# Graph attention on one core: the context is divided on VectorE, and every load and store stands between the transfers of two groups

## The reference, cut to what matters

```python
q = _heads(x @ Wq + bq); k = _heads(x @ Wk + bk); v = _heads(x @ Wv + bv)
scores = jnp.einsum('bhqd,bhkd->bhqk', q, k) / np.sqrt(64)
bias = jnp.where(adj, 0.0, -9e15)[:, None]
probs = jax.nn.softmax(scores + bias, axis=-1)
ctx = jnp.einsum('bhqk,bhkd->bhqd', probs, v)          # then heads side by side
x = _layernorm(x + (ctx @ Wf + bf), axis=-1)
```

## Time and profile before

| | |
|---|---|
| median of 3 runs | 1295.83 us (1287.64, 1295.83, 1299.62) |
| profiled execution | 1290.07 us |
| its span in the trace | 1288.3 us |
| mean granted clock of TensorE | 0.974 of full speed |
| busy: TensorE, VectorE, ScalarE, GpSimd | 92%, 76%, 63%, 44% |
| queue 1 (SyncE's), share of the 16 DMA engines | 76.7% |

### The profile page before, as it was taken

The page is one execution under the profiler, slowest core; times in us unless marked ns, Lnnn a source line. Parts: engine busy times, 40 slices in busy tenths (PEclk is TensorE's granted clock), DMA queues, the critical chain, the costliest instruction groups (busy, mean ns, idle before and its releaser), DMA issues.

```text
span 1288.3 us, 24781 instructions
## 1 busy us (share of the span) xinstructions
PE 1187.8 (92%) x8790; PEld 891.4 (69%) x8790; DVE 984.5 (76%) x1535; ACT 807.7 (63%) x1628; POOL 560.8 (44%) x943
## 2 busy tenths in 40 slices
PE   6998999899998899988999989998999889999874
PEld 5866777566776677766787667776777667786653
DVE  5788877778677886878868878688876778778782
ACT  5666765657665676666666676666775657656551
POOL 1234643446524454344543544344643436433432
PEclk9999999999998999989999999999999989999998
DMA  5688787977879777888778888789787887878784
GB/s 161 154 202 228 181 206 189 230 195 176 204 189 237 180 185 196 194 214 203 188 195 194 220 203 210 180 207 239 182 201 199 207 204 174 212 172 203 193 201 109
DMA packets 111611, 251.71 MB, mean 195 GB/s; under 512 B 27904, under 2 KB 62336, under 8 KB 111488
## 3 DMA queue, kind: packets, MB, share of 16 engines
q1 hardware_dynamic: 107296, 243.58, 76.7%
q10 hardware_dynamic: 4192, 6.56, 1.9%
HBM read 36.11 MB, written 12.58 MB: 38 GB/s over the span
## 4 chain that ended last, share of the span: by engine, by line
PE 55%; SPq 17%; DVE 12%; DMA 7%; ACT 4%; issue 4%; POOL 1%; ACTq 0%; POOLq 0%; DVEq 0%
PE context_ps L538 19%; SPq L308 16%; PE score_ps L523 13%; PE job_ps L425 7%; DMA prob_t<-prob 6%; PE job_ps L427 6%; PE job_ps L426 6%; DVE prob L735 6%; DVE prob L728 4%; ACT prob L628 3%; PE job_ps L459 2%; DVE res L750 1%; SPq L388 1%; PE job_ps L435 0%; PE score_ps L435 0%
## 5 line engine op out<-in xcount | busy, mean ns | idle before, releaser
L728 DVE CUSTOM_DVE_ANT_0 prob<-score_ps,mask 128x1024 f32<-128x1024 f32 x384 | 454.8, 1222 | 225.1 <-PE score_ps L523 163.5
L628 ACT ACTIVATE prob<-prob,row_min 128x1024 f32<-128x1024 f32 x384 | 440.2, 1148 | 213.3 <-DVE row_min L728 212.5
L735 DVE STREAM_TRANSPOSE prob<-prob 128x1024 f32<-128x1024 f32 x384 | 457.8, 1230 | 38.8 <-ACT prob L628 38.8
L538 PE MATMUL context_ps<-prob_t,v_all 128*64 128x256 f32 x3072 | 373.0, 398 | 61.9 <-DMA prob_t<-prob 61.8
L538 PEld LDWEIGHTS context_ps<-prob_t,v_all 128*64 128x64 f32 x3072 | 239.4, 144 | 166.9 <-issue 82.1
L850 POOL TENSOR_TENSOR context<-context_raw,context 128x256 f32<-128x256 f32 x96 | 70.8, 738 | 337.5 <-ACT context_raw L645 337.1
L523 PE MATMUL score_ps<-k_hi,q_hi 64*128 64x512 f32 x768 | 141.1, 445 | 4.5 <-DVE row_min L728 3.6
L425 PE MATMUL job_ps<-xt_hi,weight_hi 128*128 128x256 f32 (+1 forms) x423 | 142.0, 336 | 0.0
L427 PE MATMUL job_ps<-xt_hi,weight_lo 128*128 128x256 f32 (+1 forms) x423 | 135.6, 320 | 0.0
L426 PE MATMUL job_ps<-xt_lo,weight_hi 128*128 128x256 f32 (+1 forms) x423 | 135.5, 320 | 0.0
L523 PE MATMUL score_ps<-k_lo,q_hi 64*128 64x512 f32 x768 | 120.9, 392 | 0.0
(11 more groups left out here) (78 smaller groups left out, 1659.5 us busy)
## 6 DMA issues: line engine op xcount, KB each, us to landing
prob_t<-prob SPq DMA_DIRECT2D x1528, 128.0 KB, 2.4
res<-in_x_dram SPq DMA_DIRECT2D x32, 384.0 KB, 4.3
out_dram<-res SPq DMA_DIRECT2D x32, 384.0 KB, 2.9
adj_in<-in_adj_dram SPq DMA_DIRECT2D x31, 256.0 KB, 3.0
x_in<-in_x_dram SPq DMA_DIRECT2D x16, 384.0 KB, 3.5
x_in<-in_x_dram ACTq DMA_DIRECT2D x14, 384.0 KB, 4.5
prob_t<-prob ACTq DMA_DIRECT2D x8, 128.0 KB, 4.8
res<-in_x_dram SPq DMA_DIRECT2D x1, 768.0 KB, 6.8
```

The source lines that it names most:

```text
L538: last = pe.matmul(context_ps[64 * head:64 * head + 64, 0:GQ], v_all[:, kt, col:col + HS], keys, start=(kt == 0), stop=(kt == TT - 1))
L628: nc.scalar.activation(probabilities(t), probabilities(t), ACT.Exp, scale=-1.0, bias=row_min[:, ring:ring + 1], accum_out=row_sum[:, s // ...
L728: nc.vector.tensor_tensor_reduce(probabilities(t), in_quarters(score_ps[:, head, :]), in_quarters(mask[:, s % 2, :]), 1.0, HUGE, ALU.add, ...
L735: nc.vector.transpose(probabilities(t), probabilities(t)).then_inc(squared, 1)
```

## The change

Two things change.

First, the division of the context. ScalarE no longer copies the product out of PSUM, and GpSimd no longer multiplies: VectorE multiplies straight out of PSUM (`divide`), between the slot's two turns. The tile `context_raw` and the semaphore `context_out` go; the next mix waits for `context_done`, the end of the multiplication.

Second, the places of loads and stores. All four tables now hold even slots only, and the two x loads that ScalarE issued are entries 12 and 14 of `X_LOADS`, on SyncE's queue.

```diff
-STORES = {1: -2, 9: -1, 13: 0, 21: 1}
-RES_LOADS = {2: 0, 10: 1, 14: 2, 22: 3}
-X_LOADS = {4: (0, 0), 6: (0, 1)}
-RESIDUALS = {2: -1, 6: 0, 13: 1, 17: 2}
+STORES = {2: -2, 10: -1, 16: 0, 20: 1}
+RES_LOADS = {4: 0, 12: 1, 18: 2, 22: 3}
+X_LOADS = {4: (0, 0), 6: (0, 1), 12: (1, 0), 14: (1, 1)}
+RESIDUALS = {2: -1, 6: 0, 14: 1, 20: 2}
...
             def mix(b, group):
-                pe.wait_ge(context_out, at(b, GROUPS, group + 2))
+                pe.wait_ge(context_done, at(b, GROUPS, group + 2))
...
-            def take_context(b, group):
-                act.wait_ge(mixed, at(b, GROUPS, group + 3))
-                act.wait_ge(context_done, at(b, GROUPS, group + 2))
-                nc.scalar.activation(context_raw[:], context_ps[:, 0:GQ], ACT.Copy).then_inc(context_out, 1)
...
                     for job in slot_work(b.mode, s):
-                        if job[0] == "m":
-                            take_context(b, job[1])
-                        elif job[0] != "p" and job not in early:
+                        if job[0] not in "pm" and job not in early:
                             evict(b, job)
-                            if job == ("x", FT - 1, 0, 1):
-                                for i in range(2):
-                                    load_x(nc.scalar, b, 1, i)
...
+            def divide(b, group):
+                dve.wait_ge(mixed, at(b, GROUPS, group + 3))
+                dve.wait_ge(job_out, out_through(b, ("i", group, 0, 0)))
+                nc.vector.tensor_tensor(context[:], context_ps[:, 0:GQ], context[:],
+                                        ALU.mult).then_inc(context_done, 1)
...
                         turn_squares(b, 2 * s)
+                    for job in work:
+                        if job[0] == "m":
+                            divide(b, job[1])
+                    if s < SLOTS:
                         turn_squares(b, 2 * s + 1)
...
-            def divide(b, group):
-                pool.wait_ge(context_out, at(b, GROUPS, group + 3))
-                pool.wait_ge(job_out, out_through(b, ("i", group, 0, 0)))
-                nc.gpsimd.tensor_tensor(context[:], context_raw[:], context[:], ALU.mult).then_inc(context_done, 1)
...
                     for job in work:
-                        if job[0] == "m":
-                            divide(b, job[1])
                         if job[0] in "kqx":
                             low_part(b, job)
```

More of the change, by code:

```diff
@@ L157, in graph_attention @@
         raw = sb("raw", [P, 2, 512], F32)
-        context_raw = sb("context_raw", [P, GQ], F32)
         context = sb("context", [P, GQ], F32)
@@ L207, in graph_attention @@
         mixed = sem("mixed")
-        context_out = sem("context_out")
         context_done = sem("context_done")
@@ L419, in _ @@
             pe.sem_inc(mixed, 2)
-            pe.sem_inc(context_out, 2)
             pe.sem_inc(projected, 4)
@@ L702, in _ @@
             dve.sem_inc(masked, 2)
+            dve.sem_inc(context_done, 2)
             dve.sem_inc(sum_done, 8)
@@ L818, in _ @@
             pool.sem_inc(context_lo_done, 1)
-            pool.sem_inc(context_done, 2)
             pool.sem_inc(normalised, 4)
```

## The result

| | before | after |
|---|---|---|
| median | 1297.72 us (4 runs, 1287.64 to 1301.90) | 1260.56 us (4 runs, 1256.01 to 1262.70) |
| profiled execution | 1290.07 us | 1262.70 us |
| its span | 1288.3 us | 1260.9 us |
| mean granted clock | 0.974 | 0.982 |

The ratio is 0.972, 95% interval 0.9656 to 0.9784: faster. The forecast was 1248 with a range of 1234 to 1279. The median lies in the range, 12.6 us above the forecast. So the profiles account for 27.4 us of spans, while the medians differ by 37.2.

A forecast was written before the change was run, and what follows sets the result against it. Bound: TensorE's work plus about 12 us per element of waits for transfer landings and half clock. Six middle elements save 37 us, the last 5, element 0 nothing: 42 off 1290.1 gives 1248 us, range 1234 to 1279.

The forecast's parts named there:

- The two x loads, 3.9 us, and little when ahead of a group: Slot 11, during group 4: ScalarE's loads delay its landing 3.9 us; ahead of a group, its issue time covers them.
- rival B: x loads cost the same wherever placed: 3.9 us in seven elements, 1275 us; sign: landings over 3 us; chance 0.13.
- The store, 0.7 us: A store inside a group's transfers costs it 0.7 us, four times per element; groups 4 and 6 are on the loop.
- A clean group, 12.6 us: An undisturbed group of transfers takes 12.6 us from first issue to landing, ends 12.3 and 12.9.
- The loop walked anew, 7.6 us in element 1: Groups 4 to 7 of batch element 1 recomputed: slot 18's mix starts at 285.4 instead of 292.96, 7.6 us earlier.
- 149.7 us for a middle element: Each of six middle elements: 149.0 us from the walk, plus 0.3 for slot 8 and 0.4 for half clock.
- rival A: New waits in slots 14 and 16 drop TensorE to 1.2 GHz in each element: 20 us, 1268 us; chance 0.14.
- What an element took before doesn't matter: Middle elements: each takes 149.0 us before additions, whatever it took before, since its waits are replaced.
- Element 0 and the last, 0 and -5 us: Element 0 gains 0; the last gains 5 us, from a last turn some 4 us earlier and a shorter end.
- The multiplication, 0.45 us, almost hidden: VectorE between a slot's turns: 0.45 us, 12 per element, leaving it 0.1 us late instead of waiting.
- Rival C: SyncE's queue of all loads, stores and transfers becomes the bound: 161.5 us per element, 40 us slower, 1330; chance 0.07.
- Expected waits of 25 us: TensorE's waits for transfers fall from 61.8 to about 25 us, most in slots 14 and 16.

The follow-up runs named there:

- The queue's half alone: Kernel before with all four new tables and the x loads on SyncE's queue, division as it was: 1262.71 us, ratio 0.9753.
- the small loads: Kernel after with the x loads of slots 12 and 14 cut to 16 of their 128 partitions: 1254.93 us, ratio 0.9688.

## Why the prediction was right, and where it was off

*What bounds the kernel, and where the gain comes from*: shown. The queue's half alone gives the gain to within the noise (1262.71 against 1260.56 us), the division none. Slot 12's wait fell from 4.86 to 0.63 us in element 1 and is at most 1.1 in the other middle elements.

*The two x loads, 3.9 us, and little when ahead of a group*: shown in the main. Near the end of a group one costs 2 us; ahead of one or right behind it the mask or mix starts 1.8 to 1.9 us behind the last issue in most groups. It is not always free: the mix that waits for group 6, with two loads ahead, starts 2.9 us behind the last issue in element 1 and 3.4 in element 3. The second is over the 3 us that I had named as a sign of rival B, the only one in slots 16 and 18 of the middle elements, and with the small loads it went (though element 5 then had 3.0). The loads also cost more before than I had read: group 5, with none of them near its end, landed 3.3 to 3.8 us behind its last issue in every middle element, and 1.7 to 1.8 after the change. TensorE came later than that in five of the six and waited 1.35 us in element 5; the walk's 12.6 us for group 5 holds only because the loads went.

*The store, 0.7 us*: its size is as read, but it is not additive with the loads, by the race above.

*A clean group, 12.6 us*: right on the mean, with a spread that I had not priced. From first issue to mix or mask, groups 4, 5 and 6 of element 1 took 13.1, 12.65 and 12.9 us. The issues alone take 10.0 to 11.9 us, and SyncE starts group 6 up to 1.5 us late. A late landing costs TensorE, and an early one gives nothing back.

*The loop walked anew, 7.6 us in element 1*: 6.4 (156.6 to 150.2). Counted from the element's start, the mixes of slots 12, 14, 16 and 18 start at 78.2, 89.7, 102.1 and 114.5, where the walk had 77.8, 89.1, 100.9 and 113.3. The new waits are there as forecast, in slots 14 and 16, but the second is 2.0 us, not 1.2.

*The step that was mis-sized: 149.7 us for a middle element.* They took 151.8. TensorE's busy time in the six is 144.6 us where the clock stays up, and 9.8 us more in all because it fell in four of them. I had allowed 0.4 us for each, 2.4 in all: **7.4 us** too little. The rest, 6 x 2.1 - 7.4 = **5 us**, is idle time of TensorE: 5.6 us per element, where the walk leaves 149.3 - 144.6 = 4.7. The half clock is half of rival A: it wanted 20 us in seven elements, and the clock took about 9.8 in six. My reason against it was one wait of 1.41 us that left the clock up; waits of 2.04 (element 1) and 2.31 us did so too after the change, but one of 1.08, one of 2.26 and another of 2.04 (element 4, slot 14) ended at 1.2 GHz. The length of the wait ahead of the mix alone does not separate them, and what does stays open. The sum also leans on one profiled execution: it takes 42 us off 1290.1, and by the spans of the two profiles the gain is 27.4. That the medians differ by 37.2 helped the forecast; it was not reckoned.

*What an element took before doesn't matter*: borne out by this pair of profiles. The middle elements took 151.5 to 158.5 us before and take 149.8 to 153.6; element 5, the fast one before (151.5), lost 2.1.

*Element 0 and the last, 0 and -5 us*: -0.7 and -4.1. The 1.6 us ahead of element 0 come with a stretch of 3.4 us at 1.2 GHz, from 20.8 us on. The division-only kernel, with the old tables, had one there too, the queue's half alone too, and the one with the later x loads on ScalarE had none, so the runs tie it to neither half.

*The multiplication, 0.45 us, almost hidden*: 0.424, and the division-only kernel is at 1.0019. VectorE waits 42.0 us for mixes, 15.4 of them in the last two, where nothing else is left to do; in slots 12, 14 and 16 of element 1 it does not wait at all, and elsewhere mostly 0.24 to 0.32 us.

*Rival B* is refuted at its price of 3.9 us by the kernel with small loads; some 0.8 per element may be left of it. The rule of the Trainium skill ("DMA: Bandwidth & Descriptors", "Issuing engines are not separate DMA queues"), that a second issuer saves only the time to initiate, agrees with the times for single loads: 1262.27 against 1260.56. For a burst of 16 short transfers that saved time was the bound itself, and two of them on ScalarE's queue gave 12 us by the medians, 10.5 by the ratios.

*Rival C* was not seen: no middle element took the 161.5 us of SyncE's bound, and of 121 loads and stores on its queue 4 took over 1 us to issue. But in the loop SyncE's issue time is what remains, as the shared transfers showed.

*Expected waits of 25 us*: 45.7. Element 0 still has 5.2 us of them and the last element some 16, for which I had left little room, and the six middle ones have 4.1 each where the walk had 2.7.

## What to carry to other kernels

Where an engine waits for a burst of short transfers, look at what else is issued in the last 3 us of the burst, on another queue too: here one load on the other queue delayed the landing by 2 us, and the same load right behind the last issue left that landing alone. Then look at the next burst too, which it can delay instead. When most landings follow their last issue by the same tail (1.7 to 1.8 us here), count issues: moving two of sixteen to another engine's queue helped, and moving four made that engine's work the bound. When several cures treat one stall, expect their gains to overlap, and price the spread of a stage as well as its mean.

## What the runs showed of the hardware

An issue on SyncE usually takes 0.59 us, but in every run some take far longer. In the tile view of the changed kernel (min/median/max in ns, first and last start):

```profile
L306 SPq DMA_DIRECT2D prob_t<-prob x1528: 507/591/2135, 38.4 to 1235.0; - x191
```

Of 1649 issues behind the first 30 us, 54 took over 1.1 us, 1.58 on the mean, about half of them 22 to 27 issues apart; before it was 55 of 1635. In the middle elements 40 of the 72 groups have such an issue; they take 10.6 to 11.9 us of issues, the other 32 take 10.0 to 10.8, most of them 10.0 to 10.4. The late landings are found among those 32 alone: eight groups landed 2.6 to 3.5 us behind their last issue, and none of the 40 did. So a delay of 0.5 to 1.8 us seems to meet a group either in its issues or in its landing; that the two are one thing is not shown, and why they come is open.

ScalarE issued DMA transfers ahead of work that stands before them in its program, when their own waits were met: the x load at 262.18 above, with the evictions of 263.31 ahead of it in the program, and in the kernel before likewise the load of the earlier trace rows.
